# Causal mask products of a fused two-layer kernel: from full-height 64x128 products to 64x64 quarters

## What is computed

```python
qkv = (x @ Wqkv_w + Wqkv_b).reshape(Bb, Ll, 3, Hh, dd)
...
scores = jnp.einsum('bhid,bhjd->bhij', q, k) * scale
causal_mask = jnp.triu(jnp.full((Ll, Ll), -10000.0, dtype=scores.dtype), 1)
attn = jax.nn.softmax(scores + causal_mask, axis=-1)
y_softmax = jnp.einsum('bhij,bhjd->bhid', attn, v)
...
y = alpha * y_softmax + (1.0 - alpha) * y_stp
return y @ out_w + out_b
```

## Time and profile before

| | |
|---|---|
| runs | 2086.78 us, median of 3 (2080.41 to 2090.04) |
| profiled execution | 2081.97 us, of which the span of the profile 2080.6 us |
| granted clock of PE, mean of the span | 0.936 of 2.4 GHz |
| PE busy | 1812.6 us, 87% of the span |
| DVE, ACT, POOL busy | 1295.3, 1134.7, 660.3 us |
| chain that ended last | PE 56%, DVE 20%, issue 8%, ACT 5%, POOL 4% |

### The profile page before, as it was taken

One profiled execution on the slowest core, in us unless ns is written; L12 is line 12 of the kernel. 1 busy time (PEld: TensorE's weight loads), 2 busy tenths in 40 slices (PEclk: granted clock), 3 DMA queues, 4 the chain that ended last, 5 costly groups with the idle time before them and its releaser, 6 DMA issues.

```text
span 2080.6 us, 45291 instructions
## 1 busy us (share of the span) xinstructions
PE 1812.6 (87%) x19452; PEld 1056.7 (51%) x19472; DVE 1295.3 (62%) x2096; ACT 1134.7 (55%) x1720; POOL 660.3 (32%) x468
## 2 busy tenths in 40 slices
PE   4688879999999999999658899799889988598799
PEld 2456646776677677677522324233333423355465
DVE  5566536666666666666566776586677663555544
ACT  2365647667666766766315676566566665222221
POOL 5220004342343434235504442544444344000000
PEclk8899969999999999999858999899999999799999
DMA  6754000000000000000161532252262220000000
GB/s 166 215 132 96 7 9 1 2 1 1 2 2 1 1 2 2 1 2 2 73 148 42 161 77 50 88 137 63 82 143 62 62 63 21 0 11 6 6 11 11
DMA packets 38361, 102.08 MB, mean 49 GB/s; under 512 B 3856, under 2 KB 12176, under 8 KB 34704
## 3 DMA queue, kind: packets, MB, share of 16 engines
q1 hardware_dynamic: 38160, 99.18, 18.5%
HBM read 66.93 MB, written 31.46 MB: 47 GB/s over the span
## 4 chain that ended last, share of the span: by engine, by line
PE 56%; DVE 20%; issue 8%; ACT 5%; POOL 4%; DMA 1%; POOLq 0%; DVEq 0%; SPq 0%; ACTq 0%
PE accs L1153 8%; DVE arena L1261 4%; PE ring L1870 3%; PE accs L1934 3%; PE ring L2364 3%; PE ring L2366 3%; PE accs L2333 3%; PE ring L1896 3%; PE ring L1129 2%; PE ring L1103 2%; DVE arena L1271 2%; PE ring L1864 2%; PE ring L1835 2%; DVE arena L2023 1%; DVE arena L2063 1%
## 5 line engine op out<-in xcount | busy, mean ns | idle before, releaser
L1261 DVE TENSOR_REDUCE arena<-ring 128x2 f32<-128x1024 f32 (+2 forms) x320 | 346.1, 1112 | 148.1 <-PE ring L1110 97.2
L1375 ACT ACTIVATE arena<-ring 128x1024 f32<-128x1024 f32 (+3 forms) x384 | 304.3, 808 | 174.4 <-PE ring L1136 139.0
L1153 PE MATMUL accs<-arena 128*9 128x512 f32 (+3 forms) x1536 | 322.2, 500 | 0.0
L1129 PE MATMUL ring<-arena 51*128 51x512 bf16 (+3 forms) x768 | 133.5, 342 | 26.7 <-DVE arena L1261 14.8
L1103 PE MATMUL ring<-arena 48*128 48x512 bf16 (+3 forms) x768 | 131.5, 353 | 22.7 <-DVE arena L1261 10.0
L2248 POOL TENSOR_TENSOR arena<-arena 128x1280 f32<-128x1280 f32 x28 | 65.3, 2332 | 265.2 <-PE accs L1934 234.6
L1129 PEld LDWEIGHTS ring<-arena 51*128 51x128 bf16 x768 | 37.9, 94 | 207.0 <-issue 82.9
L2240 POOL TENSOR_TENSOR arena<-arena 128x512 f32<-128x512 f32 x112 | 138.9, 1272 | 10.2 <-DVE arena L2044 10.2
L2232 POOL TENSOR_TENSOR arena<-arena 128x1024 f32<-128x1024 f32 x32 | 75.6, 2364 | 190.2 <-DVE arena L2063 190.2
L2443 DVE TENSOR_TENSOR arena<-arena,ring 128x512 f32<-128x512 f32 x80 | 55.0, 688 | 122.7 <-PE ring L2366 112.2
L2493 ACT ACTIVATE arena<-ring 128x512 f32<-128x512 f32 x80 | 47.8, 597 | 147.0 <-PE ring L2364 147.0
(11 more groups left out here) (334 smaller groups left out, 4365.5 us busy)
## 6 DMA issues: line engine op xcount, KB each, us to landing
arena<-whole_k SPq DMA_DIRECT2D x32, 512.0 KB, 4.6
arena<-whole_q SPq DMA_DIRECT2D x32, 512.0 KB, 6.2
arena<-a_scratch_q SPq DMA_DIRECT2D x16, 384.0 KB, 6.9
arena<-a_scratch_k SPq DMA_DIRECT2D x16, 384.0 KB, 8.3
arena<-c_scratch_q SPq DMA_DIRECT2D x16, 384.0 KB, 8.2
arena<-c_scratch_k SPq DMA_DIRECT2D x16, 384.0 KB, 10.1
a_scratch_k<-arena SPq DMA_DIRECT2D x8, 512.0 KB, 3.9
c_scratch_k<-arena SPq DMA_DIRECT2D x8, 512.0 KB, 5.2
```

The source lines that it names most:

```text
L1129: mm = nc.tensor.matmul(ps[:, r * BANK:r * BANK + cols], ks[half(r, SHIFT), pair, j * P:(j + 1) * P], qs[half(r, SHIFT), pair, a:a + cols] ...
L1153: mm = nc.tensor.matmul(acc[ci % 2][32 * h:32 * h + HD + 1, a - c * BANK:BANK], c_values[b % 2][:, j, r * HEADS // 2 + 2 * g + i, :], weig ...
L1261: nc.vector.tensor_reduce(dst, src, AX.X, ALU.max, negate=True).then_inc(c_max_taken.up(item), 1)
L1375: nc.scalar.activation(view(c_probs[wi % 4]), view(ps), ACT.Exp).then_inc(c_weights_made.up(item), 1)
```

## The change

Each mask is now written only into the 64 output rows that it is for: the weights are 64 columns of `half_rows` in place of 128, and the output is the half h of the partitions of PSUM. So the four mask products of a block lie in the four 64x64 quarters of the array (r picks the rows, h the columns). Their number, their widths and their place in the order are as before, and no wait is added or taken away. `half_rows` shrinks from 256 to 64 columns, in its transfer and in its one copy by ACT. The `skip_group_check` flags only tell the builder not to look for a group of accumulation per bank.

```diff
-        "half_rows": np.concatenate([r % 64 == c, r % 64 + 64 == c], 1) * 100.0,
+        "half_rows": (r % 64 == c[:, 0:64]) * 100.0,
...
                             if diag:
-                                for r in range(2):
-                                    nc.tensor.matmul(o[r][:, width - P:width], w3["half_rows"][half(r, 64), 0:P],
-                                                     w3["causal_row"][half(r, 64), 0:P], start=False, stop=False)
-                                for r in range(2):
-                                    mm = nc.tensor.matmul(o[r][:, width - 64:width], w3["half_rows"][half(r, 64), P:2 * P],
-                                                          w3["causal_row"][half(r, 64), P:P + 64], start=False, stop=True)
+
+                                for h, first, cols in ((0, width - P, slice(0, P)), (1, width - 64, slice(P, P + 64))):
+                                    for r in range(2):
+                                        mm = nc.tensor.matmul(o[r][half(h, 64), first:width], w3["half_rows"][half(r, 64), 0:64],
+                                                              w3["causal_row"][half(r, 64), cols], start=False, stop=True,
+                                                              skip_group_check=True)
...
                         if diag:
-                            for r in range(2):
-                                nc.tensor.matmul(ps[:, r * BANK:r * BANK + 64], w3["half_rows"][half(r, 64), 0:P],
-                                                 w3["causal_col"][half(r, 64), 0:64], start=False, stop=False)
-                            for r in range(2):
-                                mm = nc.tensor.matmul(ps[:, r * BANK:r * BANK + P], w3["half_rows"][half(r, 64), P:2 * P],
-                                                      w3["causal_col"][half(r, 64), 64:64 + P], start=False, stop=True)
+                            for h, last, columns in ((0, 64, slice(0, 64)), (1, P, slice(64, 64 + P))):
+                                for r in range(2):
+                                    mm = nc.tensor.matmul(ps[half(h, 64), r * BANK:r * BANK + last],
+                                                          w3["half_rows"][half(r, 64), 0:64], w3["causal_col"][half(r, 64), columns],
+                                                          start=False, stop=True, skip_group_check=True)
```

More of the change, by code:

```diff
@@ L1103, in pe_program @@
                                 mm = nc.tensor.matmul(o[r], qs[half(r, SCORE), pair, n * P:(n + 1) * P],
-                                                      ks[half(r, SCORE), pair, a:c], start=True, stop=not diag)
+                                                      ks[half(r, SCORE), pair, a:c], start=True, stop=not diag,
+                                                      skip_group_check=True)
                             if diag:
-                                for r in range(2):
-                                    nc.tensor.matmul(o[r][:, width - P:width], w3["half_rows"][half(r, 64), 0:P],
-                                                     w3["causal_row"][half(r, 64), 0:P], start=False, stop=False)
-                                for r in range(2):
-                                    mm = nc.tensor.matmul(o[r][:, width - 64:width], w3["half_rows"][half(r, 64), P:2 * P],
-                                                          w3["causal_row"][half(r, 64), P:P + 64], start=False, stop=True)
+                                for h, first, cols in ((0, width - P, slice(0, P)), (1, width - 64, slice(P, P + 64))):
+                                    for r in range(2):
+                                        mm = nc.tensor.matmul(o[r][half(h, 64), first:width], w3["half_rows"][half(r, 64), 0:64],
+                                                              w3["causal_row"][half(r, 64), cols], start=False, stop=True,
+                                                              skip_group_check=True)
                         mm.then_inc(c_row_scored.up(item), 1)
@@ L1129, in pe_program @@
                             mm = nc.tensor.matmul(ps[:, r * BANK:r * BANK + cols], ks[half(r, SHIFT), pair, j * P:(j + 1) * P],
-                                                  qs[half(r, SHIFT), pair, a:a + cols], start=True, stop=not diag)
+                                                  qs[half(r, SHIFT), pair, a:a + cols], start=True, stop=not diag,
+                                                  skip_group_check=True)
                         if diag:
-                            for r in range(2):
-                                nc.tensor.matmul(ps[:, r * BANK:r * BANK + 64], w3["half_rows"][half(r, 64), 0:P],
-                                                 w3["causal_col"][half(r, 64), 0:64], start=False, stop=False)
-                            for r in range(2):
-                                mm = nc.tensor.matmul(ps[:, r * BANK:r * BANK + P], w3["half_rows"][half(r, 64), P:2 * P],
-                                                      w3["causal_col"][half(r, 64), 64:64 + P], start=False, stop=True)
+                            for h, last, columns in ((0, 64, slice(0, 64)), (1, P, slice(64, 64 + P))):
[3 more added lines that the diff above has]
+                                                          start=False, stop=True, skip_group_check=True)
                         mm.then_inc(c_key_scored.up(item), 1)
```

## The result

The kernel of after takes 2138.26 us (median of 6 runs, 2134.54 to 2146.29), that of before in the same series 2085.52 (6 runs): 53 us more, a ratio of 1.026 with a 95% interval of 1.0234 to 1.0285. The forecast was 2141.

What follows compares the result with a forecast made beforehand. PE's instruction stream was taken to bound stage c. Shape changes and quarters add 40 and 31 us, 71 together; less 3 and 12 hidden, 56 us, giving 2138 to 2143, predicted 2141, range 2115 to 2165.

Steps and rivals of the forecast that it cites:

- PE is the bound of the stage: Stage c, items W and M: for some 600 of 658 us nothing holds PE but its own instruction stream.
- A change of shape stalls PE by 0.09: Around the masks of stage c: each switch between 64*128 and 64*64 products costs PE some 0.09 us.
- The four quarters run beside each other: Masks of a block: four quarters take 0.058 us in place of 0.09, or 0.078 with weights not loaded ahead.
- The sum: PE in stage c: 512 blocks add 40 us, 310 followed by scores add 31 us, together 71 us more.
- What is swallowed: Stage c: 3 us hidden in the first unit, 12 us in 83 waits of PE, leaving 56 of 71 us.
- What would show it: Profile after: quarters 0.30 behind 512-column scores, scores 0.14 behind masks, V and other engines' busy times unchanged, waits some 45 us.
- quarters need no change: Rival: 64*64 products between 64*128 ones cost no stall, only the 16 us gain remains: 2072 us; chance 0.03.
- the waits swallow most: Rival: PE's lateness is made up at nearly every wait, leaving 15 to 30 us: 2102 to 2117; chance 0.09.
- stalls cost more than themselves: Rival: later tiles delay DVE and ACT, and the granted clock falls more often: 87 us more, 2174; chance 0.08.

Runs made afterwards that it cites:

- products of one column: Kernel before plus two zero-adding one-column products behind each block's masks: 2158.11 us as 64*64 quarters, 2092.64 as 64*128 (control); before 2083.81.
- the kernel with one shape throughout: Against the kernel before, all scores of stage c written as quarters as well as the masks: 2075.68 us, before 2083.81, ratio 0.996.
- items V in pairs: Kernel before, masks unchanged, planner puts two items V of different heads behind each other after every second W: 2050.10 us, before 2085.38.
- the later pairs: Kernel before, masks unchanged, items V in pairs of different heads, each pair one item W later: 2091.77 us, before 2081.32.
- pairs of the same heads: Kernel before with W taken two key tiles at a time, items V paired within the same heads: 2113.17 us; control with V alone 2086.47.

## Why the prediction was right

- **PE is the bound of the stage.** Right: DVE and POOL work as long as before, and PE's added time, 77 us busy, comes out at the end as 57 in the stage, the rest being taken from PE's idle time.
- **A change of shape stalls PE by 0.09.** Right, and now measured for the pair of shapes that had no row: 0.09 to 0.10 into quarters and 0.09 back, in the changed kernel and in products of one column.
- **The four quarters run beside each other.** Right. But the 0.03 that this was to save is not seen in a block that V follows: from the first mask to V it is 0.18 before and after. The quarters behind a change cost close to the old 0.09. Their weights are not loaded ahead: the load of L1110 starts together with its products at 1223.83, while that of L1107 before starts at 1204.63, 0.22 ahead of its products. In the kernel with one shape throughout they cost 0.04.
- **The sum.** From the traces it is 512 times 0.098 and 310 times 0.09, 50 and 28 us, 78 together, and PE's busy time grew by 77; forecast were 40 and 31, 71. The first term was sized too small by 0.02 a block: the quarters were put at 0.078, and the change into them at the low end of the three rows.
- **What is swallowed.** Forecast 15 us, 3 in the first unit and 12 in waits. The waits gave 15 (55 to 39.5), the first unit some 2 (it grew by 1.4, 30.9 to 32.3, where PE's busy time grew by 3.3). By PE's idle time it is 18 and 2 us, 20 together, so this term, too, was too small, by 5. The two errors are nearly of the same size and cancel: that the forecast came within 3 us of the time is partly luck; that the stalls of 0.09 on PE's path decide is not.
- **What would show it.** V as before, the same busy times elsewhere, clock 0.94 and above the limit of 0.92, waits 40 where 45 was said. The quarters start 0.32 behind scores of 512 columns (0.30 was said), and scores 0.17 behind the last quarter, where the text said 0.14 although its own sum holds 0.178 from the first; the sum was right and that sentence was not.
- **The rivals.** That quarters need no change is refuted by the products of one column. That the waits swallow most, and that stalls cost more than themselves, didn't come true: clock and waits moved by 0.01 and 15 us.

The Trainium skill, TensorEngine Tiling (Array Packing), section Key Properties, has the rule that a change of the tiling mode drains TensorE. The traces agree: each added change of shape costs PE some 0.09 us here.

## What to carry to other kernels

Before packing small products into quarters, count the changes of shape on both sides of them, and set each against the columns that the packing saves: here 0.09 us twice a block, for 0.02 to 0.05 saved. Packing pays when a whole run of products takes the same shape, as with all scores in quarters, and even then 8 us were all that came out here. And when an order is changed to save such stalls, look at which strips of the array neighbouring products use: two products in different strips run beside each other, which was worth more here than the stalls, up to the point where the engines behind PE set the pace.

## What was not expected

- Products of two items V in different strips overlap fully: eight in 0.98 us against four in 0.97. The kernel before leaves half the strips idle in every item V.
- The granted clock fell when PE was relieved: 0.94 to 0.96 in the kernels that PE bounds, 0.88 with items V in pairs and 0.86 with the later pairs (1100 to 1700 us), where PE is busy for 482 and 468 us of 600; with pairs of the same heads it is busy for 512, and the clock is 0.95. Part of the gain went there: the eight products of a pair take 1.63 us where the granted clock is 0.58 (1215.46 to 1217.09 in the first run with pairs), and 0.98 where it is 1.00 (1217.91 to 1218.89). How much it was in all is not shown. Busy time with the later pairs:

```profile
1100.00:1700.00 600.00, 467.89 (x4832) 188.61 (x4824) 403.55 (x439) 349.80 (x451) 262.75 (x178) 0.86 0.35 86
```
